# A recurrent and routed-experts model on one core: expert weights spread by DMA, and steps of a period set apart

## The reference, cut to what matters

```python
# 1 state-space block: 256 channels, 16 states
x_d = silu(conv4(x_d) + conv_b)                       # 4 taps
delta = softplus(dt_raw * W_dt + b_dt)
h = exp(delta * A) * h + delta * b_t * u_t ; y = sum_s h * c_t     # scan over time
# 2 routed experts: 16 experts of width 64, the best 2 by softmax, and one shared expert of 352
h = silu(g) * h ; out = einsum('nef,efd,ne->nd', h, w_down, combine) + shared * sigmoid(...)
# 3 LSTM (20 units) over time, its output steers Gaussian attention over all earlier positions
# 4 four layers of 4 experts of width 512, the best 2 by softmax
xe = layernorm(x) * g + b ; h = gelu(xe @ w1 + b1) ; y = h @ w2 + b2
x = sum_e comb[e] * (x + y[e])
```

## Time and profile before

| | |
|---|---|
| median of 3 runs | 3378.73 us (3375.25 to 3379.81) |
| the profiled execution | 3390.12 us, span 3388.3 us |
| mean granted TensorE clock | 0.777 |
| busy shares PE, DVE, ACT, POOL | 79%, 59%, 43%, 31% |
| instructions | 31,049 |
| DMA | 154.19 MB, queue of SP at 16.1% of the 16 engines |

### The profile page before, as it was taken

How to read it: one execution, slowest core, us unless ns; L and a number is a source line. 1 busy time by engine, 2 the same in 40 slices (tenths; PEclk the granted TensorE clock), 3 DMA queues, 4 the chain that set the end, 5 groups by cost and what they waited for, 6 DMA issues and landing times.

```text
span 3388.3 us, 31049 instructions
## 1 busy us (share of the span) xinstructions
PE 2668.2 (79%) x7400; PEld 1339.2 (40%) x7400; DVE 2006.7 (59%) x6745; ACT 1441.9 (43%) x4739; POOL 1050.6 (31%) x915
## 2 busy tenths in 40 slices
PE   3766784378886888778886888788878998699698
PEld 1122443244343444344433444343444444444444
DVE  4756586367765767467756776467766454444422
ACT  3231433345443555345543555345543544444333
POOL 4735256015531345125332354125431000200200
PEclk7576665569986889679885998679876997598688
DMA  3211232002211122102210122102210110011010
GB/s 108 61 51 50 65 92 63 20 2 66 72 46 25 50 53 69 35 18 72 62 38 21 50 66 59 31 13 74 63 35 2 35 41 29 4 47 38 16 50 28
DMA packets 92179, 154.19 MB, mean 46 GB/s; under 512 B 11649, under 2 KB 21368, under 8 KB 91996
## 3 DMA queue, kind: packets, MB, share of 16 engines
q1 hardware_dynamic: 91996, 152.20, 16.1%
HBM read 145.36 MB, written 6.82 MB: 45 GB/s over the span
## 4 chain that ended last, share of the span: by engine, by line
PE 43%; DVE 30%; ACT 15%; issue 9%; SPq 1%; POOL 1%; DMA 0%; DVEq 0%; ACTq 0%; POOLq 0%
PE p_hid L657 8%; DVE state L1167 8%; PE p_gates L902 6%; PE p_misc L669 4%; ACT cell_t L916 4%; PE p_acc L669 3%; DVE cell L932 3%; PE p_gate L478 3%; DVE add_c L929 3%; DVE weighed L1176 2%; PE p_misc L358 2%; DVE hist L935 2%; ACT cand L913 2%; PE p_acc L487 2%; DVE terms L823 2%
## 5 line engine op out<-in xcount | busy, mean ns | idle before, releaser
L902 PEld LDWEIGHTS p_gates<-hist,w_hh 22*128 22x128 f32 x2048 | 376.7, 228 | 1200.6 <-DVE hist L935 1057.8
L902 PE MATMUL p_gates<-hist,w_hh 22*128 22x4 f32 x2048 | 463.8, 294 | 457.2 <-DVE hist L935 451.7
L657 PE MATMUL p_hid<-xhat,w 128*128 128x512 f32 x1024 | 586.6, 656 | 0.0
L926 DVE SCALAR_TENSOR_TENSOR p_gates<-p_gates,cell 20x4 f32<-20x4 f32 x1024 | 170.7, 167 | 627.8 <-ACT p_gates L912 606.0
L916 ACT ACTIVATE cell_t<-cell 20x4 f32<-20x4 f32 x1024 | 207.7, 203 | 763.1 <-DVE cell L932 763.1
L1104 POOL TENSOR_TENSOR drive<-du,rows 128x512 f32<-128x512 f32 x256 | 455.8, 1780 | 98.3 <-DVE state L1167 77.8
L392 POOL TENSOR_TENSOR n_rstd<-n_var,minus_half 128x4 f32<-128x4 f32 x56 | 58.0, 1035 | 1360.2 <-DVE n_var L380 1360.2
L717 ACT ACTIVATE hid<-p_hid,b1f 128x512 f32<-128x512 f32 x512 | 351.8, 687 | 252.7 <-PE p_misc L669 142.5
L1167 DVE TENSOR_TENSOR_SCAN state<-decay,drive 128x512 f32<-128x512 f32 x256 | 404.1, 1579 | 27.8 <-POOL drive L1108 18.0
L1123 POOL TENSOR_TENSOR y<-y,weighed 128x512 f32<-128x512 f32 x192 | 242.5, 1263 | 514.7 <-DVE weighed L1176 513.5
L935 DVE SCALAR_TENSOR_TENSOR hist<-p_gates,cell_t 20x4 f32<-20x4 f32 x1024 | 162.7, 159 | 275.7 <-ACT cell_t L916 275.7
(11 more groups left out here) (214 smaller groups left out, 3476.7 us busy)
## 6 DMA issues: line engine op xcount, KB each, us to landing
rows<-rows_dram SPq DMA_DIRECT2D x128, 512.0 KB, 5.0
w<-w_dram SPq DMA_DIRECT2D x128, 256.0 KB, 2.7
w<-in_w2T SPq DMA_DIRECT2D x128, 256.0 KB, 2.7
w<-in_w1T SPq DMA_DIRECT2D x16, 256.0 KB, 2.7
w_dram<-w SPq DMA_DIRECT2D x16, 256.0 KB, 2.0
out_xT<-result SPq DMA_DIRECT2D x8, 256.0 KB, 2.6
xin<-in_xT SPq DMA_DIRECT2D x7, 262.0 KB, 4.2
steps<-in_c_steps SPq DMA_DIRECT2D x8, 128.0 KB, 2.9
```

Of the source, the lines that this page charges most:

```text
L657: nc.tensor.matmul(p_hid[:, v % 2, :], w1[:, v // FB, (v % FB) * P:(v % FB + 1) * P], xhat[:, :], start=True, stop=True).then_inc(g_h, 1)
L902: nc.tensor.matmul(p_gates[:, :, t:t + 1], w_hh[:, :], hist[:, :, t:t + 1], start=False, stop=False, skip_group_check=True).then_inc(gates ...
```

## The change

- Experts' weights. `choose_dve` ends with the float32 product; the split in three bfloat16 parts (four instructions) goes. PE transposes the float32 weights, ACT copies them to SBUF (`combT0`, `combT1`), SP stores them to a DRAM scratch and reads each row back to 64 or 128 partitions. The matmuls L650 and L484 and the copies L712 go.
- Terms and sums of `layer1`: the term stands at v = 6, 10, 14, its sum two slots later; both of the last expert stay at v = 17.
- `layer0`: DVE has one product in each of three steps; PE no longer waits for the weighted product before the next gate matmul.
- Decays: at offsets 21, 22, 0 (one each), 1 (two), 2, 3, 4 (one each). ACT gets a `preload_act_table(ACT.Gelu)` after the copy of `combT1` at offset 4.
- Softplus starts at slot 6 of a period instead of slot 0.
- `leave` and `pre` start 5 slots earlier, beside the last norm of `layer1` and beside each other; `pre` has 12 steps with two taps each, and uses other PSUM banks.

```diff
@@ choose_dve
-        nc.vector.tensor_scalar(half[:, :, :], tanh_[:, :, :], 0.5, 0.5, ALU.mult, ALU.add)
+        nc.vector.tensor_scalar(half[:, :, :], tanh_[:, :, :], share_of, share_of, ALU.mult, ALU.add)
...
-        dve.wait_ge(s_step, n * 9 + 7)
-        nc.vector.tensor_copy(comb3[:, :, 0:E], comb[:, :, :]).then_inc(s_step, 1)
...
-        nc.vector.tensor_tensor(comb3[:, :, 64:64 + E], crest[:, :, :], comb3[:, :, 32:32 + E], ALU.subtract).then_inc(s_comb, 1)
@@ layer0_pe
+            if u:
+                pe.wait_ge(act0_done, n)
...
-            if u < E0 // 2:
-                pe.wait_ge(act0_done, n + 1)
-                nc.tensor.matmul(p_gate[:, :], pair[:, u, :], combT0[:, :], start=True, stop=True)\
-                    .then_inc(rows_done, 1)
@@ layer0_dve
         for u in range(U0):
             n = q * U0 + u
-            yield
-
+            if u:
+                weigh(u - 1)
+            yield
             dve.wait_ge(silu_done, n + 1)
...
+            yield
             dve.wait_ge(act0_done, n + 1)
@@ layer1_pe
-            for v in range(UN + 2):
-                if v < E1:
...
-                    nc.tensor.matmul(p_acc1[:, :], pick1[:, v, :], combT1[:, :], start=True, stop=True)\
-                        .then_inc(g_rows, 1)
@@ layer1_act
-                    nc.scalar.copy(combT1[:, :], p_hid[0:96, 1, :].bitcast(BF16)[:, 0:CT]).then_inc(g_combT_taken, 1)
+                    nc.scalar.copy(combT1[:, :], p_hid[0:E1, 1, :]).then_inc(g_combT_taken, 1)
+                    act.preload_act_table(ACT.Gelu)
...
-                    act.wait_ge(g_rows, n * E1 + v + 1)
-                    nc.scalar.copy(comb_b[:, v, :], p_acc1[:, :]).then_inc(g_rows_taken, 1)
@@ layer1_dve
+                if v in (6, 10, 14):
+                    weigh((v - 6) // FB)
+                if v in (8, 12, 16):
+                    add((v - 8) // FB)
+                if v == UN + 1:
+                    weigh(E1 - 1)
+                    add(E1 - 1)
@@ layer1_sp (and likewise layer0_sp, 16 loads of 64 partitions a period)
+                if w == 0:
+                    sp.wait_ge(g_combT_taken, n + 1)
+                    sp.dma_start(comb1_dram[n % 2], combT1[:, :]).then_inc(g_comb_stored, 16)
+                if w == 1:
+                    sp.wait_ge(g_comb_stored, 16 * (n + 1))
...
+                    for k in range(2):
+                        sp.dma_start(comb_b[:, 2 * k:2 * k + 2, :], comb1_dram[n % 2, 2 * k:2 * k + 2, :].rearrange("(o e) t -> o e t", o=1)
+                                     .to_broadcast([P, 2, CT])).then_inc(g_rows_loaded[k], 16)
@@ mamba_pre_pe
+        taps(0, (0, 1))
+        yield
+        yield
+        taps(0, (2, 3))
+        yield
...
+        taps(1, (0, 1))
+        yield
+        taps(1, (2, 3))
+        yield
@@ period
+        tail = ends - 5
...
-                    advance(soft, "soft", SOFT)
+                    if layer1 is None or slot >= 6:
+                        advance(soft, "soft", SOFT)
...
-                    if o < 4:
-                        next(burst, None)
-                        next(burst, None)
...
+                if layer1 and att - 2 <= slot < tail - 2:
+                    for _ in range({21: 1, 22: 1, 0: 1, 1: 2, 2: 1, 3: 1, 4: 1}.get(o, 0)):
                         next(burst, None)
...
-            if u + 1 < NCH and slot >= ends and done["leave"] > LEAVE - 1 and (i or done["fold"] > fold_slots):
+            if u + 1 < NCH and (slot >= tail if i else done["leave"] > LEAVE - 1 and done["fold"] > fold_slots):
                 advance(pre, "pre", PRE)
```

More of the change, by code:

```diff
@@ L269, in body @@
     hid_done = sem("f0_hid_done")
-    rows_done = sem("f0_rows_done")
+    comb_stored = sem("f0_comb_stored")
+    rows0_loaded = [sem(f"f0_rows_loaded{k}") for k in range(2)]
     hidw_done = sem("f0_hidw_done")
@@ L317, in body @@
     g_combT_taken = sem("f1_combT_taken")
[L318 to L319 removed]
+    g_comb_stored = sem("f1_comb_stored")
+    g_rows_loaded = [sem(f"f1_rows_loaded{k}") for k in range(2)]
     g_h = sem("f1_h")
@@ L949, in mamba_pre_pe, with taps @@
         x = lambda k: xin[:, u % 2, :, k:k + CH]
+        def taps(j, ks):
+            for k in ks:
+                mm = nc.tensor.matmul(p_hid[:, 1 - j, :].rearrange("p (b t) -> p b t", b=B), w_tap[:, j, k, :], x(k),
+                                      start=(k == 0), stop=(k == TAPS - 1))
+            if k == TAPS - 1:
+                mm.then_inc(conv_done, 1)
         pe.wait_ge(m_prep, PREP)
@@ L997, in mamba_pre_act @@
             act.wait_ge(ssm_stored, 16 * u)
-        nc.scalar.copy(ssm[:, :], p_acc1[0:2 * S + 1, :]).then_inc(ssm_taken, 1)
+        nc.scalar.copy(ssm[:, :], p_hid[0:2 * S + 1, 1, :]).then_inc(ssm_taken, 1)
+        act.wait_ge(mz_done, u * NB + 2)
+        nc.scalar.activation(zs[:, 1, :], p_misc1[:, :], ACT.Silu).then_inc(mz_taken, 1)
         yield
-        for j, bank in ((0, p_misc1[:, :]), (1, p_hid[:, 0, :])):
+        yield
+        for j, bank in ((0, p_hid[:, 0, :]), (1, p_acc1[:, :])):
             act.wait_ge(dt_done, u * NB + j + 1)
@@ L1006, in mamba_pre_sp @@
     def mamba_pre_sp(u):
-        for _ in range(5):
+        for _ in range(8):
             yield
@@ L1373, in period @@
             o = (slot - att) % LAYER
-            heavy = layer1 is not None and slot >= att and 6 <= o < LAYER - 1 and slot < ends - 5
+            heavy = layer1 is not None and slot >= att and 6 <= o < LAYER - 1 and slot < tail
             if layer0 and not (heavy and slot < CH):
@@ L1389, in period @@
                         advance(scan, "scan", SCAN)
-                elif slot >= att and slot < ends - 5:
-                    if o < 4:
+                elif heavy:
+                    advance(scan, "scan", SCAN)
+                if layer1 and att - 2 <= slot < tail - 2:
+                    for _ in range({21: 1, 22: 1, 0: 1, 1: 2, 2: 1, 3: 1, 4: 1}.get(o, 0)):
                         next(burst, None)
-                        next(burst, None)
-                    if heavy:
-                        advance(scan, "scan", SCAN)
-                if slot >= ends and (done["scan"] > SCAN or (layer1 and done["scan"] >= SCAN)) and done["leave"] <= LEAVE:
+                if slot >= tail and (done["scan"] > SCAN or (layer1 and done["scan"] >= SCAN)) and done["leave"] <= LEAVE:
                     if done["scan"] == SCAN:
@@ L1474, in _ @@
                 load_raw(k)
-            whole(dict(pre=mamba_pre_sp, scan=mamba_scan_sp, leave=mamba_leave_sp, fold=fold_sp, layer1=layer1_sp))
+            whole(dict(pre=mamba_pre_sp, scan=mamba_scan_sp, leave=mamba_leave_sp, fold=fold_sp, layer0=layer0_sp, layer1=layer1_sp))
             sp.wait_ge(stored, NCH * 16)
```

252 lines of the change are left out of this document (136 added, 116 removed).

## The result

The changed kernel takes 3321.88 us (median of four executions, 3318.90 to 3323.12) where the one before takes 3378.81 in the same job: a ratio of 0.9831, with a 95% interval of 0.9803 to 0.9859. It is faster by 57 us, against 50 forecast.

What follows compares the result with a forecast made beforehand. No engine full; a slot lasts its other DVE or ACT work plus the LSTM's 0.97 us, or PE's queue sets it. Terms -10 - 2 - 9 - 10 - 16 - 4 = -51 gave 3329 us, own range 3300 to 3360.

Steps and rivals of the forecast that it cites:

- Offset 4: In the 20 layers with decays, reloading Exp's and Gelu's tables lengthens this slot from about 3.0 to 5.1 us: +42.
- Rival (a): Table loads decide: offset 4 costs its whole 3.2 us, tail taps at half clock, softplus hides nothing: 3385; chance 0.17.
- The other edits of the layer: In 20 layers: decays +23, -22, -6; choice of experts -12; offset 5 -13; spreading -12; evener steps -6; sums -4.
- Terms and sums: In `layer1`, separate slots save 0.1 us three times a layer: -4 us on the 20 layers.
- Spreading by DMA: In `layer1`, weights arrive 7 to 12 us after the copy, needed after 15; in `layer0` also no cost.
- rival (c): Weights come late: two loads at once take over 12 us, terms wait 3 us on 28 layers: 3413; chance 0.07.
- Periods 6 to 8: Layers without decays: -0.3 a layer, -2 us in periods 6 and 7; -2.4 a layer, -9 in period 8.
- The tail: End of a period: taps in groups of four and overlap with the norm's waits, -4 a period, -16 on four.
- Softplus: Started at slot 6, its products are partly hidden by the attention's long slots: -2 a period, -10 on five.
- The opening: The stretch ahead of period 0, priced together with period 0 at -4 us.
- Rival (b): No second load: the Exp at offset 4 costs no reload, slot stays 3.2 to 3.8 us: 3289; chance 0.14.
- Rival (d): All slots balance, DVE bounding every slot, so moved work only moves: 3378 within 7; chance 0.07.

Runs made afterwards that it cites:

- e1: The changed kernel without preload_act_table, all else as changed: 3230.4 us, ratio 0.9546.
- e2: The changed kernel with the Exp of offset 4 moved to offset 3, the preload kept: 3211.1 us, ratio 0.9488.
- e8: The changed kernel with each expert's sum in the slot of its term again: 3331.8 us, ratio 0.9856.
- e9: e2 with the preload only in periods with decays: 3205.5 us, ratio 0.9491.
- e11: The changed kernel with `pre`'s taps in two groups of eight instructions again, each in one slot: 3332.9 us, ratio 0.9869.
- e5: The changed kernel with `leave` and `pre` started after `layer1`'s last norm, as before: 3316.7 us, ratio 0.9836.
- e4: The changed kernel with softplus from slot 0 of each period, as before: 3314.5 us, ratio 0.983.
- e6: The changed kernel with `layer0`'s DVE steps as before (nothing, two products, one product), weights still by DMA: 3340.9 us, ratio 0.99.
- e7: The changed kernel with `layer0`'s gate matmul waiting again for the weighted product of the unit before: 3492.3 us, ratio 1.0357.
- e12: e9 with one Exp kept at offset 4, issued before `layer1`'s share of the slot: 3211.5 us, ratio 0.9516.

## Why the prediction was right, and where it was not

The time fell inside the forecast's own range and 7 us from its centre, but that closeness is in part luck. The layers came out 36 us above their term, and the opening and period 0 (27), the tails (16) and the attention (6) below theirs; these errors cancel. So the terms are what is to be learned.

Of the signs it named, these came: the four loads and their places, no wait for the weights' DMA, and a granted clock of 0.79 to 0.84 in the tails of periods 1 to 4. These did not: offset 4 was 6.2 us and not about 5, offset 10 still has 3.19, and the attention hid nothing of softplus.

*Offset 4* was the right mechanism with too small a size. All four loads stood where I had put them. Loads begin at 1150.98 and 1152.27 and the Exp at 1153.56, so a switch costs 1.28 to 1.29 us. The Trainium skill ("ScalarE: Activation LUTs", section "What ACT_TABLE_LOAD costs") adds a DRAIN of about 1380 ns to every switch. This trace has no room for it. I priced the slot at 5.1 us; it was 6.23 in the mean. PE's transposes, which I let cost nothing, stand ahead of the copy and the loads, and I had allowed 0.2 us of waiting for them. Here ACT waits 1.17 us for them. Over the 32 layers the four transposes take 1.0 us of PE a layer in float32 and took 0.56 in bfloat16:

```profile
L639 PE MATMUL p_hid<-ident_b,comb 128*96 128x128 bf16 x128 | 17.8, 284 | 0.0
L707 ACT COPY combT<-p_hid 96x512 bf16<-96x512 bf16 x32 | 18.6, 581 | 30.2 <-PE p_hid L639 29.8
L635 PE MATMUL p_hid<-ident,comb 128*4 128x128 f32 x128 | 32.2, 404 | 0.0
L697 ACT COPY combT<-p_hid 4x512 f32<-4x512 f32 x32 | 18.4, 574 | 58.6 <-PE p_hid L635 58.6
```

The first two rows are of before. ACT's wait ahead of its copy doubled, from 29.8 to 58.6 us, or by 0.9 us a layer. That makes +65 in place of +42. What the step left out altogether is what PE does afterwards: a third of the damage, 34 us, is at offsets 7 and 8, where PE works at a low granted clock (0.57 in the mean at offset 7, 0.88 in e1). Rival (a) had the slot's whole 3.2 us, but its place for the clock was the tail, where it did not occur.

*The other edits of the layer* gave more than I counted. e2, with only the first of the two Gelu loads and no Exp at offset 4, has layers at 1204.0, 86 below before; my terms without offset 4 sum to -52. The excess is at offsets 5 to 8. Offset 5 goes from 3.64 to 2.01, but in e2 Gelu's load has gone from it to offset 4, which is 0.74 us longer than before; in the changed kernel, where the load stays, offset 5 is 3.10, near the 0.6 that I took. Offsets 7 and 8 lose 0.55 us each, where I had counted half of PE's 0.39; offsets 9 and 10 give 0.5 of it back. Whether the copies and spread matmuls counted in full, or the higher granted clock (0.94 at offset 7 in e2, 0.85 before) did it, is not separated. By offsets, as means of the 20 layers: the Exps' move gained 1.33 at offset 0 (1.1 forecast) and cost 1.10 at offset 21 (1.16 forecast; on the 15 layer ends with a load the slot was 3.01, not 3.2). The choice of experts and one Exp took 0.56 from offset 3 (0.6). Terms and sums: 0.18 us in the first pair for 0.1, and more in the third (e8).

*Spreading by DMA* costs nothing, as forecast: rival (c) is out. `terms` (L809) waits for PE alone, 61.9 and 37.2 us over the span, never for the weights' DMA. The loads land in 4.6 us (5.0 assumed), two at once:

```profile
comb_b<-comb_dram SPq DMA_DIRECT2D x64, 512.0 KB, 4.6
rows<-comb_dram SPq DMA_DIRECT2D x128, 128.0 KB, 2.9
```

The `rows_dram` loads of the scan stay at 5.1 us, although the queue's share rises from 16.1% to 20.7%. What the DMA form gains over the bfloat16 form was not tested.

*Periods 6 to 8* were right in sign and size, -4.9 and -10.8 for -2 and -9: a preload of a set that is loaded already is a real load of 1.28 us. Without it the layers of periods 6 and 7 take 4 to 10 us less (e9), against my +0.6 a layer net, 5 us on 8 layers.

*The tail*: forecast -16, measured -32, and for the stated reason, as far as e11 goes (12 to 20 us). I feared the half clock (+2); the split taps ran at the full one (599 ns each in the mean). The overlap, 0 to -2 a period, gains nothing (e5).

*Softplus*: -10 forecast, 0 measured (e4). The step compared period 4's first slots with period 6's and charged the difference to work that could hide; it only moved. The attention's 16 us came from other edits. In e6 it takes 333.3 us, 3 to 8 above the other runs, so that much may be DVE's order in `layer0`; the rest stays open. The nearest candidate, untested, is that `layer0` reads its weights from `rows`.

*The opening* was the step that failed outright: I gave it and period 0 -4 and they gave -31. I had read the chain of the LSTM's slots and taken it for the whole kernel. In the opening there is no LSTM; PE, ACT and DVE pass each unit of `layer0` around, and the sequence of DVE's products sets its pace. 22 us are that order (e6). Some 8 stay open; the removed pair matmul, on which DVE stood 2.38 us in one unit, is the nearest candidate. The freed wait is none: with it back the opening stays at 331.2 (e7).

Rival (b), no second load, is what e1 and e2 made true: 3230 and 3211, far below the 3289 I gave it. It had -40 us for the missing loads; e1 gives -49 at offset 4, and the 34 us behind it were in nobody's price. Rival (d) is out: slots moved by up to 3.25 us.

## What to carry to other kernels

Before placing a table preload, list every activation that ACT will issue between it and its first use, and in which set each is: one foreign Exp in between turned a gain of some 20 us (e12 against e1) into a loss of 91 (e1). In a kernel whose slots are chained through three engines, price a stall twice, once for its own length and once for what TensorE's clock does behind it, and read the stages without that chain (opening, last period) separately, since another engine's order paces them. When two edits cost something only together, test each alone: both single edits here (91 and 111 us) were worth more than the whole change (57).

## What the runs showed that was not expected

- PE idled for 1.73 us in a slot of 5.9 and, after 1.43 us of work, for 1.43 us more; then it was 100% busy with a granted clock of 0.50. Without these stalls (e2) the same place kept 1.00. Over 20 layers the slots behind the stall make some 34 of e1's 85 us in the layers.
- Four float32 transposes of the weights take 1.0 us on PE in the mean, four bfloat16 ones took 0.56; the float32 spread from 4 rows takes as long as one from 128 rows (2.07 us for two at the half clock).
- Adding 50 MB of DMA (154 to 205 MB in all) hardly moved the frequent loads: 512 KB land in 5.1 us against 5.0, 256 KB in 2.7 as before.
- Moving one wait (e7) cost 170 us with no instruction added: 90 of it in the layers, 34 in the attention, 31 in periods 6 and 7 and 12 in period 0.
